# A residual U-net in fp32 halves on one core: VectorE subtracts the high part of level 0's odd maps, in GpSimd's place

## The chip, the cores and the metric

The kernel runs on one core of one Trainium2 chip. The metric is the device time of one execution in microseconds. The time before is the median of three runs, 94.34 us (94.33 to 94.56). All times in the rows below are of one profiled execution, counted from the start of its span.

## The reference, cut to what matters

The input x is 2 images of 32 channels of 64x64 in fp32. It is normalized for each channel and image, goes through a small U-net of 3x3 convolutions, and is added to the result.

```python
def basic_block(x, w1, w2, stride=1, ds=None):
    out = relu(conv3(x, w1, stride) * BN_S)
    out = conv3(out, w2, 1) * BN_S
    identity = conv1x1(x, ds, stride) * BN_S if ds is not None else x
    return relu(out + identity)

x0 = x
x = group_norm(x)                                      # mean and variance of each channel
x = basic_block(x, e0b0c1, e0b0c2)                     # level 0, 64x64
x = basic_block(x, e0b1c1, e0b1c2); f0 = x
x = basic_block(x, e1b0c1, e1b0c2, 2, e1b0ds)          # level 1, 32x32
x = basic_block(x, e1b1c1, e1b1c2); f1 = x
x = basic_block(x, e2b0c1, e2b0c2, 2, e2b0ds)          # level 2, 16x16
x = basic_block(x, e2b1c1, e2b1c2)
x = (relu(deconv2(x, dec0w) * BN_S) + f1) * BN_S
x = (relu(deconv2(x, dec1w) * BN_S) + f0) * BN_S
return x0 + x
```

## The kernel before, in words

**Layout.** Four pixels of a 2x2 block and 32 channels together fill the 128 partitions, so a 64x64 map is 32x32 blocks. A 3x3 convolution on pixels is then four 128x128 products on shifted views of blocks. The output of the first convolution of a block lies on "odd" maps (33x33, shifted by one pixel), that of the second on "even" maps.

**Two halves.** A product in fp32 is put together from fp32r halves: the high part is the value rounded to fp32r (ScalarE writes it), the low part is the value minus its high part. Each piece takes 12 products in this order: 4 of high weights with high values, 4 of low weights with high values, 4 of high weights with low values. So a piece needs its source's high part when it starts, and the low part only after 8 of 12 products.

**Pieces.** The work is cut into stages and pieces (`PIECES`); a piece is what one PSUM bank holds. Level 0 has four stages. Stage 0 (e0b0c1) is odd: pieces 0 to 5, three of 11 rows for each of 2 images, 363 elements in each partition. Stage 1 (e0b0c2) is even: pieces 6 to 9, two of 16 rows for each image, 512 elements. Stage 2 (e0b1c1) is odd again, pieces 10 to 15. Stage 3 (e0b1c2) is even, pieces 16 to 19. `last_row_read` tells up to which row a piece reads its source: an even piece reads one row beyond its own, so piece 6 (rows 0 to 15) needs rows 0 to 16, which lie in pieces 0 and 1; piece 7 needs piece 2 as well; piece 8 (second image) needs pieces 3 and 4; piece 9 piece 5.

**The engines, each with a queue of its own in program order:**
- TensorE (`block.tensor`) runs the pieces in order, L821. L787 is a product. It waits with `wait_source` (L791) for the high part, with `wait_w_lo` for the low weights, and again for the low part of its source.
- VectorE (`block.vector`), L688 to L759: for each piece it waits for the sums, evicts them from PSUM to `relu` in fp32 (L701 for odd maps, L705 and L707 for even ones), then computes the low part of the weights whose number is the piece's index (L712 and L713, the instruction is L584; piece 0 has none), and in even pieces the low part of the map too (L739, L744).
- ScalarE (`block.scalar`), L529 to L544: for each piece it rounds the evicted map to its high part (L533, L537), and then rounds the weights of index + 1 (`weights_hi`, L496).
- GpSimd (`block.gpsimd`): memsets, the low part of the normalized input's later rows (L458), and in level 0 the low part of the odd maps (L462 to L466). Behind it stands work for level 1 and the output.
- SP issues the loads. Weights k (4 and up) go to a slot that weights k-4 leave when their low part has been computed (L417).

`relu` has four slots: the eviction of an odd piece waits for the low part of the piece four before it (L693 to L695). `made_by` says which semaphore tells of a part: `hi_ready` for a high part in level 0, `lo_ready` for the low part of an odd piece there, `lo_kept` for an even one. Before stage 0 VectorE has normalized both images and set two masks (up to 18.4 us); by then the sums of the first pieces are waiting for it.

Of the kernel before, what the change touches and what calls it, by code (L numbers as in the profile page):

```python
# [27 lines left out]
F32 = mybir.dt.float32  # L28
# [3 lines left out]
ALU = mybir.AluOpType  # L32
# [60 lines left out]
class Stage:  # L93
# [17 lines left out]
STAGES = [  # L111
    Stage("e0b0c1", "odd", 0, 11),
    Stage("e0b0c2", "even", 0, 16, residual="normed"),
    Stage("e0b1c1", "odd", 0, 11),
    Stage("e0b1c2", "even", 0, 16, residual="block0"),
    Stage("e1b0c1", "down", 1, 17),
    Stage("e1b0c2", "even", 1, 16, shortcut="e1b0ds"),
    Stage("e1b1c1", "odd", 1, 17),
    Stage("e1b1c2", "even", 1, 16, shortcut="identity"),
# [48 lines left out]
def build(nc, x, consts, weights, out):  # L168
    ctx = ExitStack()
    with ctx:  # L170
# [3 lines left out]
        def sem(name):  # L174
            return ctx.enter_context(nc.semaphore(name))
# [71 lines left out]
        lo_ready = sem("lo_ready")  # L247
# [63 lines left out]
        def wait_half(engine, index, half):  # L311

            signal = made_by(PIECES[index], half)
            engine.wait_ge(signal, sum(made_by(p, half) is signal for p in PIECES[:index + 1]))
# [20 lines left out]
        def fp32_of(piece):  # L335

            if STAGES[piece.stage].kind == "dec0":
                return relu[:, piece.index % RELU_SLOTS, 0:256]
            if STAGES[piece.stage].residual is not None:
                return block0[:, piece.images[0], piece.row:piece.row + piece.rows, :]  # L340
            return blocks_in(relu[:, piece.index % RELU_SLOTS, :], piece)

        def split_of(piece, half):

            stage = STAGES[piece.stage]
            if stage.kind == "dec0":
                return up[:, half, piece.row]
            if stage.kind in ("odd", "down"):
                at = odd[stage.level][:, half, piece.images[0]:piece.images[-1] + 1,
                                      piece.row:piece.row + piece.rows, :]  # L350
                return at if len(piece.images) > 1 else at[:, 0]
            if stage.name == "e0b0c2":
                return flat_inside(half, piece.images, piece.row, piece.rows)
            if stage.name == "e1b0c2":
                return flat1_inside(half, piece.images[0])
            return even_inside(stage.level, half, piece.images, piece.row, piece.rows)
# [32 lines left out]
        def source_of_level(level, image):  # L389

            return last_piece(STAGE["e0b1c2" if level == 1 else "e1b1c2"], [image], BLOCKS[level - 1] - 1)

        LEVEL0 = [p for p in PIECES if STAGES[p.stage].level == 0 and STAGES[p.stage].kind != "dec1"]
# [37 lines left out]
        @block.gpsimd  # L431
        def _(pool):
            first = FLAT_PITCH + 1
            every = flat0.bitcast(F32).rearrange("p h i n -> p (h i) n")
            pool.memset(every[:, :, 0:first], 0.0)
            pool.memset(every[:, :, BLOCKS[0] * FLAT_PITCH + first - 1:], 0.0)
            pool.memset(every[:, :, first - 1 + FLAT_PITCH:BLOCKS[0] * FLAT_PITCH + 1:FLAT_PITCH],
                        0.0).then_inc(zeros_set, 1)
            def ground_1(lines):
                pool.memset(lines[:, :, 0:PITCH_1 + 1], 0.0)  # L440
                pool.memset(lines[:, :, (BLOCKS[1] + 1) * PITCH_1:], 0.0)
                pool.memset(lines[:, :, 2 * PITCH_1:(BLOCKS[1] + 1) * PITCH_1:PITCH_1], 0.0).then_inc(zeros_set, 1)

            ground_1(split0[:].bitcast(F32).rearrange("p h i a b n -> p (h i a b) n"))
            for v in (1, 2):
                f, b = FRONT[v], BLOCKS[v]
                maps = even[v][:].bitcast(F32).rearrange("p h i r c -> p (h i) r c")
                pool.memset(maps[:, :, 0:f, :], 0.0)
                pool.memset(maps[:, :, f + b:, :], 0.0)
                pool.memset(maps[:, :, f:f + b, 0:f], 0.0)  # L450
                pool.memset(maps[:, :, f:f + b, f + b:], 0.0).then_inc(zeros_set, 1)


            for image in range(IMAGES):
                pool.wait_ge(norm_ready, 2 * image + 2)
                pool.wait_ge(norm_hi, image + 1)
                for row, rows in LOW_ROWS:
                    pool.tensor_tensor(flat_inside(1, [image], row, rows), normed[:, image, row:row + rows, :],  # L458
                                       flat_inside(0, [image], row, rows).bitcast(F32),
                                       ALU.subtract).then_inc(norm_lo, 1)  # L460

            for piece in LEVEL0:  # L462
                if STAGES[piece.stage].residual is None:
                    wait_half(pool, piece.index, 0)
                    pool.tensor_tensor(split_of(piece, 1), fp32_of(piece), split_of(piece, 0).bitcast(F32),  # L465
                                       ALU.subtract).then_inc(lo_ready, 1)  # L466


            pool.wait_ge(summed, last_piece(STAGE["e0b1c2"], range(IMAGES), BLOCKS[0] - 1) + 1)
            ground_1(flat1.bitcast(F32).rearrange("p h i n -> p (h i) n"))  # L470

            for image in range(IMAGES):
                wait_half(pool, last_piece(STAGE["e1b0c1"], [image], 0), 1)
                pool.wait_ge(skip0_scaled, image + 1)
                pool.tensor_tensor(normed[:, image], normed[:, image], x_sb[:, image], ALU.add).then_inc(skip0_added, 1)  # L475


            wait_half(pool, source_of_level(2, IMAGES - 1), 1)
            pool.wait_ge(sides_by_dve, 2 * IMAGES)
            for q in range(4):  # L480
                i, j = q // 2, q % 2
                hi, lo = [even_inside(1, half, range(IMAGES), 0, BLOCKS[1])[:, :, i::2, j::2].bitcast(F32)
                          for half in range(2)]
                last = pool.tensor_tensor(skip1[:, i, :, j], hi, lo, ALU.add)
            last.then_inc(skip1_ready, 1)


            up_lo(pool, DEC0[1], up_lo_second)
# [83 lines left out]
        def _(dve):  # L572
# [115 lines left out]
            for piece in PIECES[:DEC0[0].index]:  # L688
                stage = STAGES[piece.stage]
# [27 lines left out]
                if stage.direct:  # L717
                    if not stage.from_bank:
                        wait_relu(dve, piece.index)
                    wait_half(dve, piece.index, 0)  # L720
                    lo, hi = split_of(piece, 1), split_of(piece, 0).bitcast(F32)
                    if stage.from_bank:

                        for one in range(len(piece.images)) if len(piece.images) > 1 else [slice(None)]:
                            last = dve.scalar_tensor_tensor(out=lo[:, one], in0=sums[:, one], scalar=0.0,  # L725
                                                            in1=hi[:, one], op0=ALU.max, op1=ALU.subtract)
                        last.then_inc(lo_direct, 1)
                    else:
                        dve.tensor_tensor(lo, fp32_of(piece), hi, ALU.subtract).then_inc(lo_direct, 1)  # L729
                elif stage.residual is not None:  # L730

                    if piece is LEVEL0[-1]:
                        side_starts()
                    wait_half(dve, piece.index, 0)
                    if stage.name == "e0b1c2":
                        for i, j in [(0, 0), (0, 1), (1, 0), (1, 1)]:
                            lo, hi = [plane_inside(half, image, i, j, piece.row // 2, piece.rows // 2)
                                      for half in (1, 0)]
                            last = dve.scalar_tensor_tensor(  # L739
                                out=lo, in0=fp32_of(piece)[:, i::2, j::2], scalar=0.0, in1=hi.bitcast(F32),  # L740
                                op0=ALU.max, op1=ALU.subtract)
                        last.then_inc(lo_kept, 1)
                    else:
                        dve.scalar_tensor_tensor(out=split_of(piece, 1), in0=fp32_of(piece), scalar=0.0,  # L744
                                                 in1=split_of(piece, 0).bitcast(F32), op0=ALU.max,
                                                 op1=ALU.subtract).then_inc(lo_kept, 1)
# [327 lines left out]
```

## Time and profile before

| | |
|---|---|
| median of three runs | 94.34 us (94.33 to 94.56) |
| profiled execution | 94.52 us, of it 92.5 us span |
| TensorE busy | 87.0 us (94%) |
| VectorE busy | 66.2 us (72%) |
| ScalarE busy | 42.9 us (46%) |
| GpSimd busy | 26.4 us (28%) |
| TensorE clock | 0.999 of full speed, mean |

An engine's busy time is the union of its instructions' spans. A matmul's record overlaps the next one's, so the rate of TensorE is read from the distance of starts. In the timeline a row that ends in xN merges N neighbours: its start is the first one's and its length reaches to the last one's end. Also VectorE's and ScalarE's records overlap: the next instruction starts some 0.1 us before the recorded end of the one before. "PEld" is TensorE's load of weights, which runs ahead of the matmuls. A bracket at the end of a row tells how long the engine was idle before and what released it.

### The profile page before, as it was taken

What the parts mean: (1) busy time and instruction counts of PE and PEld (TensorE: products, weight loads), DVE (VectorE), ACT (ScalarE), POOL (GpSimd) and SP (SyncE); (2) the same over time, 40 slices, a digit from 0 to 9 for tenths busy, and PEclk for the clock granted to TensorE, in tenths of its full rate; (3) what the DMA queues carried; (4) which work ended last, traced back from release to release, by engine and by line L of the source; (5) the groups of instructions that cost most, each with busy time, mean ns of one, the idle gap of its engine ahead of it and who ended that gap; (6) DMA issues with size and microseconds to landing.
All of it is one profiled execution on the core that took longest, in us unless ns stands there. A gap on an engine that the chain in (4) does not pass through costs nothing.

```text
span 92.5 us, 1508 instructions
## 1 busy us (share of the span) xinstructions
PE 87.0 (94%) x517; PEld 77.4 (84%) x517; DVE 66.2 (72%) x185; ACT 42.9 (46%) x88; POOL 26.4 (28%) x44
## 2 busy tenths in 40 slices
PE   5999999999999999999999999999999999999920
PEld 3678899997777799999877779989899999878920
DVE  5569979679998997466524679999766896246860
ACT  6007014076846663455403399899000599930100
POOL 7400061558770003433420003008830025000300
PEclk9999999999999999999999999999999999999999
DMA  1889800004358133710000000000000000000084
GB/s 30 255 248 353 254 22 4 7 0 101 98 175 283 51 113 113 172 62 0 0 0 0 0 4 0 0 0 0 7 0 0 0 4 0 7 0 0 19 299 136
DMA packets 4184, 6.51 MB, mean 70 GB/s; under 512 B 465, under 2 KB 2001, under 8 KB 4177
## 3 DMA queue, kind: packets, MB, share of 16 engines
q1 hardware_dynamic: 4176, 6.42, 22.5%
q8 instruction: 4, 0.07, 0.3%
q14 instruction: 4, 0.02, 0.1%
HBM read 5.37 MB, written 1.05 MB: 69 GB/s over the span
## 4 chain that ended last, share of the span: by engine, by line
PE 77%; DVE 14%; ACT 3%; issue 2%; DVEq 0%
PE psum L787 65%; PE psum L814 8%; DVE split L739 3%; DVE shared L729 2%; ACT split L533 2%; DVE block L707 2%; ACT shared L509 1%; PE psum L901 1%; DVE shared L674 1%; DVE result L777 1%; DVE shared L658 1%; DVE shared L701 1%; DVE shared L667 1%; DVE relu L701 1%; PE psum L965 1%
## 5 line engine op out<-in xcount | busy, mean ns | idle before, releaser
L465 POOL TENSOR_TENSOR odd<-relu,odd 128x363 fp32r<-128x363 f32 x12 | 12.1, 1009 | 17.4 <-ACT odd L537 17.4
L787 PE MATMUL psum<-shared,w_e0b0c 128*128 128x364 f32 x72 | 12.7, 332 | 0.1
L787 PEld LDWEIGHTS psum<-shared,w_e0b0c 128*128 128x128 f32 x72 | 11.9, 188 | 0.6 <-DVE shared L630 0.3
L787 PE MATMUL psum<-shared,w_e0b1c 128*128 128x364 f32 x72 | 12.2, 329 | 0.0
L787 PEld LDWEIGHTS psum<-shared,w_e0b1c 128*128 128x128 f32 x72 | 12.1, 188 | 0.1
L701 DVE SCALAR_TENSOR_TENSOR relu<-psum,inside 128x363 f32<-128x363 f32 (+2 forms) x18 | 8.8, 491 | 4.6 <-PE psum L787 4.6
L787 PE MATMUL psum<-odd,w_e0b0c 128*128 128x512 f32 x48 | 11.9, 410 | 0.0
L787 PE MATMUL psum<-odd,w_e0b1c 128*128 128x512 f32 x48 | 11.9, 410 | 0.0
L537 ACT ACTIVATE odd<-relu 128x363 fp32r<-128x363 f32 x12 | 6.2, 519 | 11.0 <-DVE relu L701 11.0
L787 PEld LDWEIGHTS psum<-odd,w_e0b0c 128*128 128x128 f32 x48 | 9.1, 190 | 2.5
L787 PEld LDWEIGHTS psum<-odd,w_e0b1c 128*128 128x128 f32 x48 | 9.1, 190 | 2.5
L814 PE MATMUL psum<-zeros 128*128 128x256 bf16 x46 | 9.0, 357 | 1.1 <-DVE eps L636 1.1
L814 PEld LDWEIGHTS psum<-zeros 128*128 128x128 bf16 x46 | 5.4, 130 | 2.7 <-DVE eps L636 1.1
L475 POOL TENSOR_TENSOR normed<-normed,x_sb 128x1024 f32<-128x1024 f32 x2 | 4.8, 2396 | 5.7 <-DVE shared L729 5.7
L458 POOL TENSOR_TENSOR shared<-normed,shared 128x352 fp32r<-128x352 f32 (+1 forms) x4 | 3.2, 815 | 10.9 <-DVE normed L600 10.9
L787 PE MATMUL psum<-shared,w_e1b0c 128*128 128x256 f32 (+1 forms) x36 | 5.6, 301 | 0.1
L509 ACT ACTIVATE shared<-even 64x180 fp32r<-64x180 f32 (+1 forms) x5 | 1.9, 386 | 7.8 <-DVE even L725 7.7
L533 ACT ACTIVATE split<-block 128x256 fp32r<-128x256 f32 x8 | 3.0, 430 | 5.0 <-DVE block L707 5.0
L787 PEld LDWEIGHTS psum<-shared,w_e1b0c 128*128 128x128 f32 x36 | 4.9, 190 | 0.5 <-DVE shared L729 0.3
L564 ACT ACTIVATE skip<-normed 128x128 f32<-128x128 f32 x16 | 5.2, 413 | 0.0
L501 ACT ACTIVATE shared<-split 32x512 fp32r<-32x512 f32 x8 | 5.0, 631 | 0.1
L707 DVE SCALAR_TENSOR_TENSOR block<-block,psum 128x512 f32<-128x512 f32 x4 | 2.8, 688 | 2.9 <-PE psum L787 2.9
(127 smaller groups left out, 146.8 us busy)
## 6 DMA issues: line engine op xcount, KB each, us to landing
out<-result SPq DMA_DIRECT2D x3, 256.0 KB, 2.6
x_sb<-x_in SPq DMA_DIRECT2D x4, 160.0 KB, 3.8
raw<-e0b0c_in SPq DMA_DIRECT2D x2, 256.0 KB, 4.8
raw<-e0b1c_in SPq DMA_DIRECT2D x2, 256.0 KB, 5.0
raw<-e1b1c_in SPq DMA_DIRECT2D x2, 256.0 KB, 2.6
raw<-e2b1c_in SPq DMA_DIRECT2D x2, 256.0 KB, 2.6
raw<-e1b0c_in SPq DMA_DIRECT2D x1, 448.0 KB, 3.9
raw<-e2b0c_in SPq DMA_DIRECT2D x1, 448.0 KB, 3.3
```

The source lines that it names most:

```text
L458: pool.tensor_tensor(flat_inside(1, [image], row, rows), normed[:, image, row:row + rows, :], flat_inside(0, [image], row, rows).bitcast(F32),
L465: pool.tensor_tensor(split_of(piece, 1), fp32_of(piece), split_of(piece, 0).bitcast(F32), ALU.subtract).then_inc(lo_ready, 1)
L475: pool.tensor_tensor(normed[:, image], normed[:, image], x_sb[:, image], ALU.add).then_inc(skip0_added, 1)
L501: last = act.activation(*corner_copy(level, image, q), ACT.Copy)
L509: last = act.activation(target, source, ACT.Copy)
L533: last = act.activation(planes_inside(0, piece.images[0], i, piece.row // 2, piece.rows // 2), fp32_of(piece)[:, i::2].rearrange("p r (c b ...
L537: act.activation(split_of(piece, 0), fp32_of(piece), ACT.Relu).then_inc(hi_ready, 1)
L564: last = act.activation(target, source, ACT.Copy)
L701: last = dve.scalar_tensor_tensor(out=target, in0=sums, scalar=0.0, in1=mask, op0=ALU.max, op1=ALU.mult)
L707: last = dve.scalar_tensor_tensor(out=target, in0=block0[:, image, rows, :], scalar=0.0, in1=sums, op0=ALU.max, op1=ALU.add)
L787: last = pe.matmul(target, w, moving, start=(first and n == 0), stop=(final and n == len(terms) - 1), skip_group_check=skip)
L814: pe.matmul(psum[:, bank, 0:256], zeros[:, 0:P], zeros[:, 0:256], start=True, stop=True)
```

## The change

GpSimd no longer subtracts the high part of level 0's twelve odd pieces. VectorE does it, in its own loop: after the eviction of a piece and the low part of the weights, and ahead of the next eviction, it waits for ScalarE's rounding of that piece, then subtracts. The operation, the operands and the semaphore that is raised are the same.

```diff
@@ block.gpsimd
-            for piece in LEVEL0:
-                if STAGES[piece.stage].residual is None:
-                    wait_half(pool, piece.index, 0)
-                    pool.tensor_tensor(split_of(piece, 1), fp32_of(piece), split_of(piece, 0).bitcast(F32),
-                                       ALU.subtract).then_inc(lo_ready, 1)
@@ block.vector
-                elif stage.residual is not None:
+                elif stage.residual is None:
+                    wait_half(dve, piece.index, 0)
+                    dve.tensor_tensor(split_of(piece, 1), fp32_of(piece), split_of(piece, 0).bitcast(F32),
+                                      ALU.subtract).then_inc(lo_ready, 1)
+                else:
 
                     if piece is LEVEL0[-1]:
                         side_starts()
```

## Rows read from the trace of the kernel before

**Rows 1.** The page: busy us (share of span) and instructions of each engine
```profile
PE 87.0 (94%) x517; PEld 77.4 (84%) x517; DVE 66.2 (72%) x185; ACT 42.9 (46%) x88; POOL 26.4 (28%) x44
```

**Rows 2.** The chain that ended last, in order of time: start us, us, what
```profile
12.32 38.41 PE psum L787 x196
...
50.75 0.70 DVE block L707
```

**Rows 3.** Timeline, 18.4 to 22 us: start us, us, engine line op out<-in xcount
```profile
18.39 0.54 DVE L701 SCALAR_TENSOR_TENSOR relu<-psum,inside 128x363 f32<-128x363 f32 x1
18.85 0.52 DVE L701 SCALAR_TENSOR_TENSOR relu<-psum,inside 128x363 f32<-128x363 f32 x1
18.96 0.53 ACT L537 ACTIVATE odd<-relu 128x363 fp32r<-128x363 f32 x1 [3.55 <-DVE relu L701]
19.39 0.61 ACT L496 ACTIVATE w_e0b0c<-raw 128x512 fp32r<-128x512 f32 x1
19.91 0.50 ACT L537 ACTIVATE odd<-relu 128x363 fp32r<-128x363 f32 x1
...
20.49 1.31 POOL L465 TENSOR_TENSOR odd<-relu,odd 128x363 fp32r<-128x363 f32 x1
20.85 11.94 PE L787 MATMUL psum<-odd,w_e0b0c 128*128 128x512 f32 x48
```

**Rows 4.** Stage 2's start; windows: stretch, its length, busy PE, PEld, DVE, ACT, POOL
```profile
32.63 3.68 PE L787 MATMUL psum<-shared,w_e0b1c 128*128 128x364 f32 x21
20.90:32.70 11.80, 11.80 (x50) 9.15 (x49) 11.09 (x18) 7.80 (x15) 5.33 (x5) 1.00 0.46 139
32.70:44.70 12.00, 12.00 (x74) 12.00 (x73) 7.47 (x13) 6.06 (x13) 4.32 (x5) 1.00 0.31 89
```

**Rows 5.** Weight subtractions: ns min/median/max, first and last start; a meeting with GpSimd in the timeline
```profile
L584 DVE SCALAR_TENSOR_TENSOR w_e0b1c<-raw,w_e0b1c x2: 945/948/952, 21.4 to 22.7; 128x512 fp32r<-128x512 f32 x2
L584 DVE SCALAR_TENSOR_TENSOR w_e1b1c<-raw,w_e1b1c x2: 684/684/685, 29.2 to 31.2; 128x512 fp32r<-128x512 f32 x2
63.43 2.03 DVE L729 TENSOR_TENSOR shared<-relu,shared 128x289 fp32r<-128x289 f32 x1
62.74 2.40 POOL L475 TENSOR_TENSOR normed<-normed,x_sb 128x1024 f32<-128x1024 f32 x1 [5.33 <-DVE shared L729]
```

**Rows 6.** Timeline: VectorE's subtracts of other sizes, each with the next instruction
```profile
9.27 0.56 DVE L630 TENSOR_TENSOR shared<-normed,shared 128x384 fp32r<-128x384 f32 x1
9.74 1.34 DVE L591 BATCH_NORM_STATS2 stats<-x_sb 128x6 f32<-128x320 f32 x3
...
62.20 0.46 DVE L729 TENSOR_TENSOR shared<-relu,shared 128x289 fp32r<-128x289 f32 x1
62.58 0.45 DVE L701 SCALAR_TENSOR_TENSOR shared<-psum,inside 128x289 fp32r<-128x289 f32 x1
```

**Rows 7.** Timeline: later evictions, a rounding and its subtract; load of weights 9 to landing
```profile
26.62 0.68 DVE L705 TENSOR_TENSOR block<-normed,psum 128x512 f32<-128x512 f32 x1
27.33 0.64 ACT L537 ACTIVATE shared<-block 128x512 fp32r<-128x512 f32 x1 [0.76 <-DVE block L705]
27.99 0.70 DVE L744 SCALAR_TENSOR_TENSOR shared<-block,shared 128x512 fp32r<-128x512 f32 x1 [0.38 <-ACT shared L537]
32.83 0.69 DVE L705 TENSOR_TENSOR block<-normed,psum 128x512 f32<-128x512 f32 x1 [0.17 <-PE psum L787]
...
raw<-e2b0c_in SPq DMA_DIRECT2D x1, 448.0 KB, 3.3
```

**Rows 8.** Timeline: TensorE's starts behind a wait, and the matmuls that follow
```profile
60.85 0.46 DVE L674 CAST shared<-split 32x580 fp32r<-32x580 f32 x1
61.45 0.37 PE L787 MATMUL psum<-shared,w_e1b0c 128*128 128x290 f32 x1
...
8.27 0.40 PE L787 MATMUL psum<-shared,w_e0b0c 128*128 128x364 f32 x1
8.51 0.50 PE L787 MATMUL psum<-shared,w_e0b0c 128*128 128x364 f32 x2
```

## The prediction

> **What bounds the kernel now.** I read the page's busy shares first [rows 1], then the chain of work that ended last [rows 2], then the timeline around the first stage boundary [rows 3], because the shares alone can't say whose wait is the last one. TensorE is busy 94% of the span at full clock. The chain shows why that is the bound for the first half: from 12.32 to 50.73 us it is one unbroken run of 196 matmuls that waits for nothing. Only behind 50.73 does it change between VectorE, ScalarE and TensorE, and it starts there from the sums of a matmul piece. So in level 0 nothing off TensorE costs time until it makes TensorE wait; once it does, everything behind moves by the same amount, since no wait stands in the chain in which it could be made up.
>
> GpSimd's subtract is none of the chain's work. Its low part of piece 1 is ready at 20.49 + 1.31 = 21.80 us [rows 3]; TensorE reaches the low terms of piece 6, which read it, after 8 of its 12 products, at 20.85 + 8 x 0.245 = 22.81 (48 matmuls fill the 11.78 us from 20.85 to 32.63) [rows 3, 4]. A faster low part is worth nothing to TensorE: it already comes 1.0 us early at the tightest place.
>
> **What is removed.** Twelve GpSimd subtracts; that engine is busy 28% of the span [rows 1]. They cost VectorE something today: its weight subtraction of the same 128x512 takes 0.945 to 0.952 us beside them and 0.68 us where GpSimd is idle [rows 5], so in stage 0 I take 0.68. GpSimd's next work after the removed loop waits for the last piece of stage 3 (L469), so it comes no earlier. Gain on the chain: 0.
> The largest such meeting in the trace is a VectorE tensor_tensor that took 2.03 us instead of 0.46, beside a GpSimd add of 2.40 us [rows 5]. The Trainium skill, SBUF — State Buffer, "Who interferes with whom", says that a VectorE instruction with two SBUF inputs contends with a GpSimd instruction that reads SBUF, and that the loser is blocked for the whole instruction. By that rule GpSimd's removal gives VectorE a block back for each weight subtraction; by the rows of this stage it is 0.27 us each. Neither reaches the chain, so the sum is the same by both.
>
> **What is added: twelve subtracts of 128x363 in VectorE's queue.** None is in the trace. The nearest rows are the same operation on 289 elements, 0.46 us with the next start 0.38 later, and on 384 elements, 0.56 us with the next 0.47 later [rows 6]. Between them, 363 elements hold VectorE 0.45 us (bounds 0.38 and 0.47). A cost below nothing is excluded: the instruction is new on this engine. With no GpSimd instruction beside it the 2.03 us row doesn't apply.
>
> **What is added: a wait.** The subtract stands in VectorE's order after the weight subtraction of its piece and in front of the next eviction (L701), and waits for ScalarE's rounding. Piece 0 has no weight subtraction (L712 asks for an index above 0), so there nothing fills the wait, and queued behind it is the eviction of piece 1. This is the one place where it costs. Step by step from [rows 3]:
> - Eviction of piece 0 at 18.39, as now. ScalarE rounds it from 18.96 to 19.49.
> - The subtract starts 0.03 us later, at 19.52 (as L744 starts at 27.99 behind a rounding that ended at 27.33 + 0.64 = 27.97 [rows 7]), and frees VectorE at 19.97.
> - Eviction of piece 1 from 19.97 to 20.50; now it starts at 18.85. So it is 1.12 us later.
> - ScalarE starts its rounding 0.03 to 0.04 later, at 20.54. Now it starts at 19.91, because the rounding of weights 1 stood in front of it until then: that hid 0.50 of the 1.12. It ends at about 21.05 instead of 20.41, 0.64 later.
> - Piece 6, first of stage 1, reads rows 0 to 16, so it needs the rounded piece 1. How long from a ready signal to the first matmul, when TensorE stands and waits? At L674 the last side copy ends at 60.85 + 0.46 = 61.31 and the matmul starts at 61.45: 0.14 [rows 8]. So piece 6 starts at 21.19 to 21.20 instead of 20.85: 0.34 later. The present slack is thus 0.30 of the 0.64.
> - A standing TensorE has the first product's spacing longer. The matmul that starts at 8.27 behind a wait has the second at 8.51, 0.24 later, where the next two come 0.17 apart (two records of 0.33 together reach over 0.50) [rows 8]. I take 0.08 more for piece 6.
> Sum: 0.34 + 0.08 = 0.42 us. Its bounds: a subtract of 0.38 and a restart at 0 give 0.27; a subtract of 0.47 and a restart twice as dear give 0.52.
>
> **The other eleven subtracts, and what hides them.** Weights 1 are subtracted from 20.42 to 21.10; TensorE wants them after four products, at 21.83 + 0.42. Piece 1's subtract starts when its rounding ends, about 21.08, and frees VectorE at 21.53 (its result about 21.62, wanted at 22.81 + 0.42). From there a piece costs VectorE 0.45 (eviction) + 0.60 (weights) + 0.45 = 1.5, up to 1.9 with the 896-wide weights, 0.5 of it new: it falls behind. Evictions of pieces 2, 3, 4, 5 come at about 21.5, 23.1, 24.6 and 26.5 (0.5 to 1.2 later than now), rounded pieces 2, 4, 5 at 22.6, 25.7 and 27.6. TensorE wants piece 2 at 20.85 + 2.95 + 0.42 = 24.2, piece 4 at 27.2 and piece 5 at 30.1 [rows 3, 4, 7]. The smallest margin is 1.5 us. The backlog then is 1.5 us at piece 6 (28.1 for 26.62) and shrinks, since in stage 1 a piece costs VectorE some 2.0 us (0.60 + 0.60 + 0.60 and the wait for the rounding) and comes every 2.95; at piece 9 the eviction is at about 34 for 32.83. In stage 2 a piece comes every 2.0 us and VectorE needs 1.5 for one; it is busy 7.5 of 12.0 us there now [rows 4], and six more subtracts make it 10.2: caught up by piece 12 or 13. Cost: 0. If that cover were gone, each late rounding would be paid in full.
> SP's loads of weights k wait for the subtraction of weights k-4. Those come up to 1.0 us later (weights 5 at 27.7 for 26.7). Weights 9 then land near 27.7 + 3.3 = 31.0, and ScalarE asks for them at about 33.3 [rows 7]: 0. ScalarE's own queue gets nothing new; it only is asked later.
>
> **The forecast.** The profiled execution took 94.52 us, 92.5 of it span; the sum is 94.94 against it. It is 0.18 above the median of the three runs, 94.34, to which the same 0.42 gives 94.76. A difference under about 0.3% (0.28 us) can't be told from no change here.
>
> **Rivals.**
> - *Mostly hidden.* The delay of the rounding is real, but TensorE's slack is larger than 0.30, or the longer first spacing is absorbed. For it: the sum is a difference of small steps, and its low bound is 0.27. Against: the signal-to-matmul row is a direct reading. Price 0.1 to 0.28, about 94.55. Chance 0.20.
> - *VectorE becomes the bound.* In 20.90 to 32.70 it is busy 11.1 of 11.8 us already [rows 4]. If the weight subtractions keep 0.95 us though GpSimd is gone (if something else slows them), and the subtract holds VectorE 0.65 instead of 0.45, piece 6 starts 0.2 later still, 0.65 in all, and the rounding of piece 4 comes at about 27.2, just when TensorE wants it: the point from which every further delay is paid again at pieces 8 and 9. Price 0.65 to 1.0, about 95.1. Against: the 512-wide ones where GpSimd is idle all took 0.68 [rows 5], and the bounds of the subtract are 0.38 and 0.47. Chance 0.11. The Trainium skill, Perfetto Trace Analysis, "Optimizing Scalar/DVE Operations", speaks against the change in the same sense: where VectorE is saturated, work may be moved off it to ScalarE or even GpSimd, and it adds that between VectorE and GpSimd this might not help because of the shared port.
> - *Faster.* The relief of 0.27 us on each of VectorE's weight subtractions in stage 0, or the earlier low parts, shorten a wait of TensorE. It would need such a wait between 12.32 and 50.73, and the chain has none [rows 2]; or a different order behind 50.73, where the relieved instructions are long over. At the most one 0.3 us wait: 94.0. Chance 0.05.
> That the order is not what the diff says I give nothing: the subtract stands in the loop ahead of the next eviction.
>
> **How the numbers follow.** Chances: 0.64 for the forecast (+0.28 to +0.55), 0.20, 0.11, 0.05. Faster by over 0.3%: 0.05. Within: 0.20. Slower by over 0.3%: 0.75. The range goes from the middle of the hidden case, 94.5, to the beginning of VectorE as bound, 95.1; outside lie the faster case, a part of the hidden one and the worse half of the second rival, together under 0.2.
>
> **What the profile of the changed kernel would show.** Right: a gap of about 0.35 us in TensorE at 20.85, with the first matmul on odd near 21.2 and "ACT odd L537" as the releaser; VectorE idle about 0.6 us between the eviction of piece 0 and the new subtract; eviction of piece 1 near 19.97; weight subtractions of 512 elements at 0.68 in stage 0; no other gap up to about 51.15, where the chain leaves TensorE. Wrong: no gap at 20.85, or a second one before piece 8 (about 27.2) or 9 (30.1), or a new subtract much over 0.54 us.

## The result, and the profile after

| | before | changed |
|---|---|---|
| median of 20 runs each, us | 94.39 (94.29 to 94.78) | 94.72 (94.48 to 94.94) |
| ratio, runs paired in time | | 1.0027 (95%: 1.0017 to 1.0037) |
| profiled execution: time, span, us | 94.52, 92.5 | 94.88, 93.1 |
| VectorE busy | 66.2 us | 70.8 us |
| GpSimd busy | 26.4 us | 14.3 us |

The changed kernel is 0.25 us slower by the ratio. Lines after the edit have moved: a product is now L785, the eviction L695, the rounding L531, the weight subtraction L578, the new subtract L726.

The timeline of the changed kernel from 18.5 to 26.8 us (start us, us, engine line op, and in brackets the idle time before it and its releaser):

```profile
18.56 0.54 DVE L695 SCALAR_TENSOR_TENSOR relu<-psum,inside 128x363 f32<-128x363 f32 x1
19.13 0.52 ACT L531 ACTIVATE odd<-relu 128x363 fp32r<-128x363 f32 x1 [3.54 <-DVE relu L695]
19.68 0.54 DVE L726 TENSOR_TENSOR odd<-relu,odd 128x363 fp32r<-128x363 f32 x1 [0.59 <-ACT odd L531]
20.14 0.53 DVE L695 SCALAR_TENSOR_TENSOR relu<-psum,inside 128x363 f32<-128x363 f32 x1
20.70 0.52 ACT L531 ACTIVATE odd<-relu 128x363 fp32r<-128x363 f32 x1 [0.54 <-DVE relu L695]
21.36 12.03 PE L785 MATMUL psum<-odd,w_e0b0c 128*128 128x512 f32 x48 [0.19 <-ACT odd L531]
21.67 0.42 PE L785 MATMUL psum<-odd,w_e0b0c 128*128 128x512 f32 x1
...
25.40 0.52 ACT L531 ACTIVATE odd<-relu 128x363 fp32r<-128x363 f32 x1 [0.22 <-DVE relu L695]
26.73 0.53 DVE L695 SCALAR_TENSOR_TENSOR relu<-psum,inside 128x363 f32<-128x363 f32 x1
28.29 0.68 DVE L699 TENSOR_TENSOR block<-normed,psum 128x512 f32<-128x512 f32 x1
```

This is the place of [rows 3]. VectorE evicts piece 0, stands 0.59 us until ScalarE has rounded it, subtracts, and only then evicts piece 1. ScalarE rounds weights 1 in the meantime and then stands idle for 0.54 us in front of piece 1, where in the kernel before it went from weights 1 straight to piece 1, and TensorE waits for the rounded piece 1. The bracket counts its idle time from the modelled end of the last matmul; by starts, the wait is longer. The last matmul row is the second product: 0.31 behind the first. In the kernel before the first two starts of this stage are 20.85 and 21.08 us, 0.23 apart:

```profile
21.08 0.42 PE L787 MATMUL psum<-odd,w_e0b0c 128*128 128x512 f32 x1
```

The chain of the changed kernel (start us, us, what) now goes through this place, and behind it is one unbroken run of matmuls up to 62.01 us:

```profile
18.56 0.55 DVE relu L695
19.10 0.02 issue
19.13 0.53 ACT odd L531
19.66 0.02 issue
19.68 0.54 DVE odd L726
20.22 0.46 DVE relu L695
20.68 0.02 issue
20.70 0.53 ACT odd L531
21.22 0.14 issue
21.36 40.65 PE psum L785 x204
```

The new instruction and the weight subtractions of stage 0 in the changed kernel (duration ns min/median/max, first and last start us), beside [rows 5]; and its busy time in stages 1 and 2 (stretch, its length, then busy PE, PEld, DVE, ACT, POOL), beside [rows 4]:

```profile
L726 DVE TENSOR_TENSOR odd<-relu,odd x12: 532/540/541, 19.7 to 46.6; 128x363 fp32r<-128x363 f32 x12
L578 DVE SCALAR_TENSOR_TENSOR w_e0b1c<-raw,w_e0b1c x2: 679/680/681, 22.1 to 23.7; 128x512 fp32r<-128x512 f32 x2
```
```profile
21.30:33.20 11.90, 11.84 (x48) 9.24 (x49) 11.30 (x21) 7.06 (x14) 0.00 (x0) 1.00 0.47 138
33.20:45.20 12.00, 12.00 (x73) 11.97 (x72) 10.91 (x20) 7.25 (x14) 0.00 (x0) 1.00 0.29 89
```

The weight subtractions fell from 0.95 to 0.68 us and VectorE is fuller; neither shows in TensorE's starts, whose only longer distances between 20 and 61 us are those at 21.36.

**Two measures for one result.** A profiled span also holds a start that differs from run to run: the matmul pair that sums the statistics of the second image starts at 11.98 us in the profile of before, at 12.14 in that of the changed kernel and at 11.78 in a second one of it.

```profile
11.98 0.33 PE L807 MATMUL psum<-result,same_channel 128*128 128x72 f32 x2
12.14 0.33 PE L805 MATMUL psum<-result,same_channel 128*128 128x72 f32 x2
```

So below I count from the first matmul of that pair (L807 before, L805 after) to the first product on odd, and to the end of the span. Before: 8.87 and 80.51 us. Changed: 9.21 and 80.95 us. Inside of the span the change costs 0.43 to 0.44 us. In the total it costs 0.25. TensorE's mean granted clock isn't the reason for either: it was 0.999 before, and 0.993, 0.989 and 1.000 in three profiles with the change's order, which agree in 80.94 or 80.95 us from the pair to the end. The experiments are about both numbers.

### The profile page after: what moved, and what is told of

Same layout as the page of the kernel before. It is cut to its first block, busy times and chain, and to the rows that moved or that the text cites. A ratio compares the mean times of both kernels' runs of the same rounds, so it can differ in the third digit from the quotient of the medians.

```text
span 93.1 us, 1508 instructions
## 1 busy us (share of the span) xinstructions
PE 87.1 (94%) x517; PEld 77.3 (83%) x517; DVE 70.8 (76%) x197; ACT 43.2 (46%) x88; POOL 14.3 (15%) x32
## 4 chain that ended last, share of the span: by engine, by line
PE 74%; DVE 10%; DMA 5%; issue 3%; ACT 2%; SPq 2%; DVEq 0%
PE psum L785 70%; DMA raw<-e0b0c_in 5%; DVE normed L594 2%; PE psum L899 1%; SPq L410 1%; DVE shared L624 1%; DVE result L775 1%; ACT odd L531 1%; DVE relu L695 1%; PE psum L812 1%; PE psum L963 1%; ACT w_e0b0c L490 1%; DVE even L704 1%; DVE odd L726 1%; DVE inside L634 1%
## 5 line engine op out<-in xcount | busy, mean ns | idle before, releaser
L785 PE MATMUL psum<-shared,w_e0b0c 128*128 128x364 f32 x72 | 12.8, 333 | 0.4 <-ACT w_e0b0c L490 0.4
L785 PEld LDWEIGHTS psum<-shared,w_e0b0c 128*128 128x128 f32 x72 | 11.8, 188 | 1.0 <-issue 0.6
L785 PE MATMUL psum<-odd,w_e0b0c 128*128 128x512 f32 x48 | 12.0, 412 | 0.2 <-ACT odd L531 0.2
L785 PE MATMUL psum<-shared,w_e0b1c 128*128 128x364 f32 x72 | 12.2, 329 | 0.0
L785 PEld LDWEIGHTS psum<-shared,w_e0b1c 128*128 128x128 f32 x72 | 12.1, 188 | 0.1
L785 PE MATMUL psum<-odd,w_e0b1c 128*128 128x512 f32 x48 | 11.9, 410 | 0.0
L785 PEld LDWEIGHTS psum<-odd,w_e0b0c 128*128 128x128 f32 x48 | 9.0, 190 | 3.0 <-issue 0.5
L531 ACT ACTIVATE odd<-relu 128x363 fp32r<-128x363 f32 x12 | 6.2, 520 | 11.3 <-DVE relu L695 11.3
L785 PEld LDWEIGHTS psum<-odd,w_e0b1c 128*128 128x128 f32 x48 | 9.1, 190 | 2.5
L695 DVE SCALAR_TENSOR_TENSOR relu<-psum,inside 128x363 f32<-128x363 f32 (+2 forms) x18 | 8.8, 491 | 0.9 <-PE psum L785 0.9
L726 DVE TENSOR_TENSOR odd<-relu,odd 128x363 fp32r<-128x363 f32 x12 | 6.5, 539 | 1.0 <-ACT odd L531 1.0
L785 PE MATMUL psum<-shared,w_e1b0c 128*128 128x256 f32 (+1 forms) x36 | 5.6, 301 | 0.1
L785 PEld LDWEIGHTS psum<-shared,w_e1b0c 128*128 128x128 f32 x36 | 4.9, 190 | 0.5 <-DVE shared L723 0.3
L737 DVE SCALAR_TENSOR_TENSOR split<-block,split 128x128 fp32r<-128x128 f32 x16 | 3.6, 289 | 1.7 <-ACT split L527 1.6
```

The costliest lines, as they stand in the source:

```text
L531: act.activation(split_of(piece, 0), fp32_of(piece), ACT.Relu).then_inc(hi_ready, 1)
L695: last = dve.scalar_tensor_tensor(out=target, in0=sums, scalar=0.0, in1=mask, op0=ALU.max, op1=ALU.mult)
L726: dve.tensor_tensor(split_of(piece, 1), fp32_of(piece), split_of(piece, 0).bitcast(F32), ALU.subtract).then_inc(lo_ready, 1)
L737: last = dve.scalar_tensor_tensor(out=lo, in0=fp32_of(piece)[:, i::2, j::2], scalar=0.0, in1=hi.bitcast(F32), op0=ALU.max, op1=ALU.subtract)
L785: last = pe.matmul(target, w, moving, start=(first and n == 0), stop=(final and n == len(terms) - 1), skip_group_check=skip)
```

## Experiments

Theory A is the prediction's: only the place of piece 0's subtract costs, and it costs all that is seen. Its first rival, Theory B, has the load on VectorE cost. Theory C is about the profiled run alone.

Each kernel was timed in turn with the kernel before on the same chip, in three groups on three chips after the first comparison. The row of before is of the first group; in the other two its mean span is 92.48 and 92.50 us and the time outside 2.06 and 2.04. Distance and pair to end are of one profiled execution of each kernel, the other numbers of all its runs. "Distance" is from the pair to the first product on odd, as above (the expectations count it from the pair's row in the chain, which is 0.16 us later: their 8.71 and 9.05 are 8.87 and 9.21 here). "Outside" is an execution's time less its span, a mean over the runs.

| kernel | what it is | distance | pair to end | mean span | outside | ratio to before (95%) |
|---|---|---|---|---|---|---|
| before (29 runs) | | 8.87 | 80.51 | 92.48 | 2.03 | 1 |
| changed (20) | | 9.21 | 80.95 | 92.90 | 1.80 | 1.0027 (1.0017 to 1.0037) |
| after_again (11) | changed, again | 9.20 | 80.94 | 92.86 | 1.79 | 1.0016 (1.0004 to 1.0028) |
| defer0 (12) | piece 0's subtract behind eviction 1 | 8.87 | 80.52 | 92.51 | 1.81 | 0.9979 (0.9966 to 0.9992) |
| twice0 (6) | piece 0's subtract twice | 9.65 | 81.35 | 93.37 | 1.79 | 1.0070 (1.0053 to 1.0087) |
| only0 (11) | only piece 0's moved | 9.20 | 80.91 | 92.81 | 1.80 | 1.0012 (1.0001 to 1.0022) |
| pool0 (12) | all but piece 0's moved | 8.87 | 80.52 | 92.38 | 1.81 | 0.9965 (0.9953 to 0.9978) |
| masks_late (6) | changed, masks set later | 8.87 | 81.19 | 93.17 | 1.81 | 1.0049 (1.0033 to 1.0066) |
| before_late (9) | before, GpSimd's add later | 8.87 | 80.22 | 92.18 | 2.02 | 0.9963 (0.9948 to 0.9978) |
| defer0_late (6) | defer0, add later | 8.87 | 80.22 | 92.23 | 1.80 | 0.9949 (0.9931 to 0.9968) |
| pool_minus1 (10) | before, one GpSimd memset fewer | 8.87 | 80.51 | 92.47 | 1.79 | 0.9974 (0.9955 to 0.9993) |
| pool_plus12 (10) | changed, 12 GpSimd memsets more | 9.21 | 80.94 | 92.85 | 2.03 | 1.0034 (1.0012 to 1.0056) |
| dve_plus1 (10) | before, one VectorE memset more | 8.87 | 80.51 | 92.56 | 2.03 | 1.0006 (0.9986 to 1.0025) |
| before_late_minus1 (6) | before, add later, one memset fewer | 8.87 | 80.22 | 92.08 | 1.82 | 0.9939 (0.9915 to 0.9962) |

### The changed kernel once more

> The changed kernel once more, as the base for its neighbours. Theory A (order: the eviction of piece 1 waits behind piece 0's subtract and its rounding) expects a gap in TensorE in front of the first product on odd, that product 9.05 us behind the start of the second L805/L807 matmul pair (before: 8.71), the next one 0.30 behind it instead of 0.23, and 0.25 to 0.43 us more than the kernel before. Theory B (load: the eleven other subtracts cost as well) expects further gaps of TensorE between 22 and 50 us. Theory C (start: the longer time of the profiled run is a late first load) expects this profile to have the gap at the first odd product but a span nearer to 92.9 than to 93.1.

The gap is there again, with the product's distance at 9.20, the second matmul 0.31 later, and no other gap up to the end of level 0. Its pair starts 0.37 us earlier than in the first profile of this kernel, and its span is 92.7 for 93.1: Theory C is right about the profiled run. The total is only 0.15 us over the kernel before, though the span is 0.38 longer in the mean. The 0.25 to 0.43 us that were expected of the total didn't come. That pointed to the time outside of the span: 1.76 to 1.84 us in all of these 11 runs, 1.95 to 2.10 in the 29 of the kernel before.

### Piece 0's subtract behind the eviction of piece 1

```diff
+            def subtract(piece):
+                wait_half(dve, piece.index, 0)
+                dve.tensor_tensor(split_of(piece, 1), fp32_of(piece), split_of(piece, 0).bitcast(F32),
+                                  ALU.subtract).then_inc(lo_ready, 1)
...
+                if piece.index == 1:
+                    subtract(PIECES[0])
                 if 0 < piece.index < len(WEIGHTS):
                     weights_lo(piece.index)
...
                 elif stage.residual is None:
-                    wait_half(dve, piece.index, 0)
-                    dve.tensor_tensor(split_of(piece, 1), fp32_of(piece), split_of(piece, 0).bitcast(F32),
-                                      ALU.subtract).then_inc(lo_ready, 1)
+                    if piece.index > 0:
+                        subtract(piece)
```

> All twelve subtracts on VectorE, but piece 0's one stands behind the eviction of piece 1 in place of ahead of it, in the time in which VectorE waits for the rounding of weights 1. Theory A expects all of the loss gone: first odd product 8.71 us behind the second L805/L807 pair, no gap, time within 0.1 us of the kernel before, ratio 0.999 to 1.001. Theory B expects that most of the loss stays (ratio 1.002 or more), since VectorE has the same work. The eviction of piece 2 comes at about 21.1, 0.1 to 0.2 later than before.

The timeline of this kernel:

```profile
18.53 0.98 DVE L700 SCALAR_TENSOR_TENSOR relu<-psum,inside 128x363 f32<-128x363 f32 x2
19.66 0.54 DVE L673 TENSOR_TENSOR odd<-relu,odd 128x363 fp32r<-128x363 f32 x1
20.04 0.50 ACT L531 ACTIVATE odd<-relu 128x363 fp32r<-128x363 f32 x1
20.99 2.36 PE L791 MATMUL psum<-odd,w_e0b0c 128*128 128x512 f32 x9
```

VectorE evicts pieces 0 and 1 in one go, subtracts for piece 0 in the time in which it stood idle anyway, and TensorE shows no idle time in front of its product. The distance and the rest of the span are those of the kernel before, with all twelve subtracts on VectorE. Theory B is out. The total is 0.2 us *below* the kernel before, which Theory A didn't expect; the span isn't (92.51 for 92.48).

### Piece 0's subtract twice

```diff
                 elif stage.residual is None:
                     wait_half(dve, piece.index, 0)
+                    if piece.index == 0:
+                        dve.tensor_tensor(blocks_in(skip0[:].rearrange("p n i j a b -> p (n i j a b)"), piece),
+                                          fp32_of(piece), split_of(piece, 0).bitcast(F32), ALU.subtract)
                     dve.tensor_tensor(split_of(piece, 1), fp32_of(piece), split_of(piece, 0).bitcast(F32),
                                       ALU.subtract).then_inc(lo_ready, 1)
```

> The changed kernel with piece 0's subtract done twice (the first into a tile that isn't in use yet), so that the eviction of piece 1 comes another 0.45 us later. Theory A expects the whole dose on the time, since the slack is used up: 0.45 us over the changed kernel, ratio to the kernel before 1.0075 (0.70 us), first odd product 9.5 us behind the second L805/L807 pair. Theory B expects a twelfth of it or nothing: below 0.1 us over the changed kernel.

```profile
19.43 0.54 DVE L727 TENSOR_TENSOR skip<-relu,odd 128x363 f32<-128x363 f32 x1 [0.58 <-ACT odd L531]
19.89 0.53 DVE L729 TENSOR_TENSOR odd<-relu,odd 128x363 fp32r<-128x363 f32 x1
20.34 0.53 DVE L695 SCALAR_TENSOR_TENSOR relu<-psum,inside 128x363 f32<-128x363 f32 x1
21.56 1.71 PE L788 MATMUL psum<-odd,w_e0b0c 128*128 128x512 f32 x6 [0.62 <-ACT odd L531]
```

The eviction is 0.45 us later still, and the idle time of TensorE grows from 0.18 to 0.62: the dose comes out whole (distance +0.44 over the changed kernel, mean span +0.5, ratio 1.0070 against 1.0016 in the same runs).

### Only piece 0 moved, and all but piece 0 moved

only0, against the kernel before:

```diff
-                if STAGES[piece.stage].residual is None:
+                if STAGES[piece.stage].residual is None and piece.index > 0:
...
+                elif piece.index == 0:
+                    wait_half(dve, 0, 0)
+                    dve.tensor_tensor(split_of(piece, 1), fp32_of(piece), split_of(piece, 0).bitcast(F32),
+                                      ALU.subtract).then_inc(lo_first, 1)
                 elif stage.residual is not None:
```

pool0, against the changed kernel:

```diff
+            wait_half(pool, 0, 0)
+            pool.tensor_tensor(split_of(PIECES[0], 1), fp32_of(PIECES[0]), split_of(PIECES[0], 0).bitcast(F32),
+                               ALU.subtract).then_inc(lo_first, 1)
...
+                elif piece.index == 0:
+                    pass
                 elif stage.residual is None:
```

In both, piece 0's low part has a semaphore of its own, which TensorE waits for in piece 6.

> The kernel before with piece 0's subtract alone on VectorE, ahead of the eviction of piece 1; GpSimd keeps the other eleven. Theory A expects the whole loss of the changed kernel (0.25 to 0.45 us, first odd product 9.05 us behind the second L805/L807 pair). Theory B expects hardly any of it, at most 0.05 us. If GpSimd's work beside VectorE matters for the loss, this kernel's weight subtractions of 512 elements take 0.95 us again and the time differs from the changed kernel's by more than 0.1 us.

> The changed kernel with piece 0's subtract back on GpSimd; VectorE has the other eleven. Theory A expects the kernel before's time: ratio 0.999 to 1.001, first odd product 8.71 us behind the second L805/L807 pair, no gap. Theory B expects eleven twelfths of the loss, 0.2 to 0.4 us. It also shows whether the moved eleven gain anything: Theory A says no, since their low parts came 1 us early before.

With one instruction moved the whole gap is there (distance 9.20, pair to end 80.91); with the other eleven moved there is none (8.87, 80.52). The place decides, not the number. In only0 GpSimd works again and VectorE's later weight subtractions take 0.95 to 0.99 us, which makes no difference to TensorE. Both expectations were wrong in the total. only0 lost 0.11 us by the ratio in place of 0.25 to 0.45: its span is 0.33 us longer in the mean, but the time outside fell here too (1.80 for 2.03). pool0 didn't take the time of the kernel before but 0.33 us less by the ratio: 0.25 us outside of the span and 0.1 in the mean span. That 0.1 is probably the scatter of the start, since from the pair to the end its profile takes what before takes.

### Masks set later

```diff
-            masks([1, 2])
             for piece in PIECES[:DEC0[0].index]:
                 stage = STAGES[piece.stage]
+                if piece.index == 16:
+                    masks([1, 2])
```

> The changed kernel with the masks of levels 1 and 2 set after stage 2 in place of ahead of stage 0, so that VectorE begins its evictions up to 2.6 us earlier (near 16 us). Theory A expects the loss gone, because the rounded piece 1 then comes over 1 us ahead of TensorE, and no more than that: ratio 0.999 to 1.001, since TensorE is the bound up to 50.7 us. If there were a gain in being early, it would be below 0.999.

Half of this came out; the total is a miss. The eviction of piece 0 moved to 15.75 us, the gap at the first odd product is gone, and being early gave nothing: the distance is 8.87 to the last digit, as TensorE's own work sets it. But the ratio is 1.0049. The 2.6 us of memsets fell into VectorE's wait in front of the eviction of piece 16, which is shorter than that: it came at 49.20 us, where it stands at 47.80 in the kernel before. This kernel's chain leaves TensorE at 44.90 us and runs over the memsets, this eviction and ScalarE into level 1, where TensorE waits (timeline of this kernel):

```profile
46.60 0.49 DVE L634 MEMSET inside<- 128x289 f32 x2
49.20 0.69 DVE L702 SCALAR_TENSOR_TENSOR block<-block,psum 128x512 f32<-128x512 f32 x1
59.77 2.25 PE L786 MATMUL psum<-split,w_e1b0c 128*128 128x290 f32 x15 [0.30 <-ACT split L527]
```

So VectorE has no cover for 2.6 us in front of piece 16. Another row shows the price of a meeting with GpSimd: the first subtract starts while GpSimd still subtracts for the input, and takes 1.03 us for 0.54.

```profile
15.91 1.59 POOL L458 TENSOR_TENSOR shared<-normed,shared 128x352 fp32r<-128x352 f32 x2 [2.32 <-DVE normed L594]
16.87 1.03 DVE L727 TENSOR_TENSOR odd<-relu,odd 128x363 fp32r<-128x363 f32 x1 [0.59 <-ACT odd L531]
```

### GpSimd's add behind piece 21

```diff
             for image in range(IMAGES):
-                wait_half(pool, last_piece(STAGE["e1b0c1"], [image], 0), 1)
+                wait_half(pool, last_piece(STAGE["e1b0c1"], [IMAGES - 1], 0), 1)
```

> The kernel before, with GpSimd's first add of 128x1024 (L475) waiting for the low part of piece 21 instead of piece 20, so that it doesn't stand beside VectorE's L729 at 63.43 us. Theory: that L729 took 2.03 us because of GpSimd's add, and TensorE waits 0.2 us for it. Expected: L729 0.46 us, no gap of TensorE at 65.2 to 65.5, 0.1 to 0.25 us less than the kernel before (ratio 0.9975 to 0.999). The rival, that the length is only VectorE's wait for something else, expects the 2.03 us unchanged.

> Both: all twelve subtracts on VectorE with piece 0's behind the eviction of piece 1, and GpSimd's first add behind piece 21. Expected the same as the kernel before with the late add, 0.1 to 0.25 us less than the kernel before, if the two places don't touch each other.

The kernel before with the later add, to be read against the 2.03 us of [rows 5]:

```profile
63.42 0.46 DVE L729 TENSOR_TENSOR shared<-relu,shared 128x289 fp32r<-128x289 f32 x1
64.47 0.43 DVE L710 TENSOR_SCALAR odd<-psum 128x256 fp32r<-128x256 f32 x1 [0.59 <-PE psum L787]
63.96 4.75 POOL L475 TENSOR_TENSOR normed<-normed,x_sb 128x1024 f32<-128x1024 f32 x2 [6.56 <-DVE shared L729]
```

The subtract takes 0.46 us as soon as GpSimd's add isn't beside it, and the rest of the span shrinks by 0.29 us (80.22 for 80.51), in both kernels. So the length was the meeting with GpSimd. The gain is larger than the 0.1 to 0.25 us that were expected: by the ratio 0.35 us for before_late. defer0_late gains 0.48 us in the total, because its time outside of the span is the lower one as well (1.80 for 2.02).

### What lies outside of the span

Nine kernels had shown two levels, 2.03 and 1.80 us, with nothing between. The two at 2.03 (before, before_late) have 44 GpSimd instructions on their page, the others 43 or fewer, but they also differ in VectorE's number. These edits tell it apart, in this order pool_minus1 (before), pool_plus12 (changed) and dve_plus1 (before); before_late_minus1 is the first of them with the later add:

```diff
-                pool.memset(maps[:, :, 0:f, :], 0.0)
-                pool.memset(maps[:, :, f + b:, :], 0.0)
+                if v == 2:
+                    pool.memset(maps[:, :, 0::f + b, :], 0.0)
+                else:
+                    pool.memset(maps[:, :, 0:f, :], 0.0)
+                    pool.memset(maps[:, :, f + b:, :], 0.0)
```
```diff
+        idle_tile = sb("idle_tile", [P, 12])
...
+            for n in range(12):
+                pool.memset(idle_tile[:, n:n + 1], 0.0)
             pool.wait_ge(summed, last_piece(STAGE["e0b1c2"], range(IMAGES), BLOCKS[0] - 1) + 1)
```
```diff
+                if piece.index == 13:
+                    dve.memset(quad_mask, 0.0)
                 if 0 < piece.index < len(WEIGHTS):
```

> The kernel before with one GpSimd instruction fewer: the two memsets of level 2's border rows are one memset with a stride; nothing else changes. What is open: the time outside of the span is 2.03 us for the kernel before (49 runs) and 1.80 us for the changed kernel and all its neighbours, while inside of the span the change costs more than it does in the total. Theory P (the length of GpSimd's program): 1.80 us outside here, the span unchanged, so 0.23 us less than the kernel before (ratio 0.9976). Theory V (the length of VectorE's program, or work on the chip): 2.03 us outside and ratio 1.000.

> The changed kernel with twelve memsets of one column into a tile that nobody reads added to GpSimd, where the twelve subtracts stood, with no wait; GpSimd is idle there. Theory P: the time outside of the span goes back from 1.80 to 2.03 us, the span stays, so the whole loss of the change is seen in the total: 0.40 to 0.48 us over the kernel before (ratio 1.0045 to 1.005). Theory V: 1.80 us outside, ratio near 1.002 as for the changed kernel.

> The kernel before with one VectorE instruction more, a memset of four columns in its idle time in stage 2. Theory P: 2.03 us outside of the span, ratio 1.000. Theory V: 1.80 us outside, ratio 0.9976.

> The kernel before with GpSimd's first add behind piece 21 and with one memset fewer; all subtracts stay on GpSimd. If the two gains have nothing to do with the moved subtracts, this is as fast as the best so far: 94.0 us, ratio 0.994 to 0.996, 1.80 us outside of the span (Theory P), L729 at 0.46 us. If moving the subtracts has a gain of its own, it stays above that by more than 0.1 us.

The page's busy lines of pool_minus1, pool_plus12 and dve_plus1, whose numbers outside are 1.79, 2.03 and 2.03 us:

```profile
PE 85.8 (93%) x517; PEld 76.6 (83%) x517; DVE 66.3 (72%) x185; ACT 43.0 (46%) x88; POOL 26.3 (28%) x43
```
```profile
PE 86.2 (93%) x517; PEld 76.7 (83%) x517; DVE 70.7 (76%) x197; ACT 43.1 (47%) x88; POOL 14.6 (16%) x44
```
```profile
PE 85.7 (92%) x517; PEld 76.6 (83%) x517; DVE 66.3 (72%) x186; ACT 42.9 (46%) x88; POOL 26.4 (28%) x44
```

One GpSimd instruction fewer takes 0.25 us from the time with nothing changed in the span (pair to end 80.51). Twelve more put it back onto the changed kernel, whose loss is then 0.33 us in the total (0.11 to 0.53 by the interval) and 0.35 in the mean span; 0.40 to 0.48 was expected, which lies in the interval but above the measured ratio. One more on VectorE does nothing. All 13 kernels fall to one side or the other by their GpSimd count, 44 or at most 43. What the device does in these 0.23 us isn't in the trace and stays open, and so does whether the count as such matters or the place of something in the program behind it.

before_late_minus1 is the fastest: 93.86 us, ratio 0.9939. It has both gains with all subtracts left on GpSimd, and from the pair to the end it takes the 80.22 us of defer0_late, so moving them has no gain of its own.

## Why the prediction was right, point by point

**The path.** That the eviction of piece 1 gets behind piece 0's wait and subtract, that ScalarE's present work on weights 1 hides 0.5 of it, and that TensorE has 0.3 of slack: each step came out. Counted from the eviction of piece 0, which came 0.17 later in this profile:

| step | predicted | measured |
|---|---|---|
| subtract starts | +1.13 | +1.12 (19.68) |
| eviction of piece 1 starts | +1.58 | +1.58 (20.14) |
| rounding of piece 1 starts, ends | +2.15, +2.66 | +2.14, +2.66 (21.22) |
| from there to the first product | 0.14 | 0.14 |
| first product later than before | 0.34 | 0.34 to 0.35 |
| second product later, on top | 0.08 | 0.08 |
| sum inside of the span | 0.42 | 0.43 to 0.44 |

**The cost of an operation that the trace lacked.** 363 elements took 0.54 us and held VectorE 0.46, between the rows of 289 and 384 [rows 6]. The removal gave 0.27 us back on each weight subtraction of stage 0, as far as [rows 5] had it.

**The cover of the other eleven.** The rounding of piece 4 ended at 25.92 us, 1.4 us ahead of piece 8's first product (21.36 + 0.08 + 2 x 2.945 = 27.33); predicted 1.5. The backlog at piece 6 was 28.29 for 26.62 + 0.16, 1.5 us as predicted. VectorE was seen to wait for TensorE again at piece 13 (41.44 us); twelve or thirteen was said. It was fuller in stage 2 than said, 10.9 us of 12.0 for 10.2.

**The rivals.** VectorE didn't become the bound: both of its conditions failed (0.68, not 0.95; 0.46, not 0.65). "Mostly hidden" failed in the span. By the ratio alone one could take it for the one that came true: 0.25 us lies in its price of 0.1 to 0.28, and below the +0.28 at which the forecast begins. But its mechanism isn't there, as neither step was hidden. The rival "faster" asked for a wait of TensorE that isn't there, and pool0 shows there is none.

**A sign that was wrong.** The chain was said to leave TensorE at about 51.15 us, as [rows 2] has it at 50.73. In the changed kernel it stays there until 62.01. It also stays there, from 12.53 to 61.63, in pool_minus1, whose order of work on TensorE and VectorE is that of the kernel before. So behind 50.7 us two paths end at nearly the same time, and the chain of one profile shows only one of them.

**What failed** is the step from the profiled execution to the total: "the sum is 94.94 against it", and the same 0.42 on the median. It took what lies around the span as fixed, and the change takes 0.23 us from it. So 0.43 became 0.25 by the ratio, 0.27% (0.17% to 0.37%) and 0.16% in the repetition. My 0.75 for slower by over 0.3% was put on the right sign, but the total lies at or below that line. That the median of 94.72 comes so near to 94.76 is in part luck: the medians of the two sets differ by 0.33 us, the paired ratio gives 0.25, and a term of 0.23 us was missing from the sum.

## What to carry to other kernels

An instruction with a wait on another engine costs its queue the wait on top of its duration (here 0.59 and 0.46 us): ask which instruction stands behind it and who waits for that one, most of all at the first turn of a loop, where the filler that covers the wait later (here the weights' low part) is missing. Put behind the next eviction, as in defer0, the same instruction cost nothing in the span. Where a change of a few tenths of a microsecond is judged, compare spans, stretches inside of the span and the time outside of it separately; a total can mix a loss on the chip's engines with a gain that has nothing to do with where the work stands.

## What the runs showed of the hardware that I had not expected

- The time outside of the span had two levels, 2.03 and 1.80 us, each run within 0.1 us of its kernel's mean over 6 to 29 runs, and one GpSimd instruction in 44 switched between them.
- A TensorE that stood waiting has its second product 0.31 us behind the first instead of 0.23 (512 columns), in all four kernels in which it waited there.
- VectorE's subtract of two SBUF tensors took 2.03 us for 0.46 beside a GpSimd add of 2.40 us, and 1.03 for 0.54 beside a GpSimd subtract. In both, GpSimd had started first and took its usual time, and VectorE's subtract ended 0.3 to 0.4 us behind it (65.46 behind 65.14 us, 17.90 behind 17.50). The Trainium skill, SBUF — State Buffer, "Who interferes with whom", has a VectorE instruction with two SBUF inputs contend with a GpSimd instruction that reads SBUF, calls the shared port pair an exclusive lock, and says (of VectorE's 2-port modes) that whoever issues first holds it for the whole instruction. These two cases agree with that.
- In stage 0 it was otherwise: VectorE's weight subtractions of 512 elements took 0.95 us for 0.68, and GpSimd's subtracts beside them 1.01 to 1.41 us where those in stage 2 take 0.91. There both engines lost a part, which isn't what a lock held for the whole instruction would give. Why, no run here shows.
